# One attention unit's V products: one key tile in every key tile, in place of two in every second

## The chip, the cores and the metric

The kernel runs on one core of one Trainium2 chip. The metric is the device time of one execution in microseconds (us). The kernel before took 1166.23 us in the median of three runs (1156.73 to 1166.93).

## The reference: what is computed

The block is `x + attention(xn) + ffn(xn)` with `xn` the layer norm of `x`, which is 4 x 1024 x 128 in float32. The part that matters here is the attention:

```python
xq, xk, xv = rope(q @ Wq), rope(kv @ Wk), kv @ Wv          # q = kv = xn
xk, xv = jnp.repeat(xk, 2, axis=-1), jnp.repeat(xv, 2, axis=-1)
scores = softmax(xq @ xk * scale, axis=-1)                 # 16 heads, 1024 x 1024 each
out = (scores @ xv).transpose(0, 2, 1, 3).reshape(batch, seq_len, -1)
return out @ Wo
```

The feed-forward part (a SiLU gate with 384 hidden columns) is computed once, at the kernel's start, and is not touched.

## The kernel before, in words

**Units.** The four batches and four groups of four heads make 16 steps; a step has two halves of 512 queries. One half of one step is a unit: 32 units, numbered `u`. Units 0 to 30 run through `slot`, the last one through `last_slot`. The keys of a unit are eight key tiles `kt` of 128 keys.

**What TensorE (PE) does in a unit**, written out by hand in `slot` (L544 to L663), key tile by key tile:
- `score(kt, h)` (L554): one matmul for each head h = 0 to 3, keys in rows and queries in columns, 98 x 128 weights, 512 columns. It alternates between the two halves of `bank_s`, so it waits until ScalarE has taken the exponential of the score two before (L553).
- `maxima()` (L391): one max tile, two matmuls into `scores`, for the row maxima of the unit after this one. Sixteen of them are spread over key tiles 0 to 5. There are two places, so max tile m waits until VectorE has reduced max tile m - 2 (L388).
- `pv(u, kt, n)` (L406): the V products of one key tile. Four heads, each with weights of 128 x 32, each in its own 32 columns of the array and its own 32 partitions of `bank_o`; in the profile every head is two instructions, so one key tile has 8. They accumulate over the eight key tiles of a unit; the first waits until `bank_o` of the unit before has been read (L404).
- `denominators(u - 1)` (L416, L419) in key tile 2: eight products with ones, in the same 128 x 32 shape; `transpose_den` and `transpose_inv` (L426, L433) in key tiles 3 and 5; `project_out(u - 2)` (L442) in key tile 1; `transpose_max` (L398) in key tile 6, one 128 x 32 weight load, which waits for `o_done` (L649); and the projections of unit u + 4 (`project_chunk`, L373, and `project_v`, L381) in key tiles 6 and 7.

**Where the V products stand.** `pv_pair` runs in key tiles 0, 2, 4 and 6. In key tile 0 it issues key tiles 6 and 7 of the unit before, in 2, 4 and 6 the two key tiles just finished.

**The other engines.** ScalarE (ACT) takes 32 exponentials (L867) into `prob`, a ring of four key tiles; before it writes a ring place it waits until the V products of the key tile four before are done (L854) and until the sums that read the place are done. Between the exponentials it copies `bank_o` to `o_raw` (`read_o`, L828), `bank_m` to `y_part` (`read_y`, L845) and other things. VectorE (DVE) reduces 16 max tiles (L946), then splits the maxima (L952, L954), normalises `o_raw` (L1049, which gives `o_done`), adds two key tiles of `prob` (L1039) and rotates the projections (L937 to L941). GpSimd (POOL) splits two chunks (L1125), adds one output (L1189) and sums `prob` over key tiles in five additions (L1173, L1181). SyncE (SP) issues the DMAs; it copies a new V after `pv_done` of the unit before (L322).

Of the kernel before, what the change touches and what calls it, by code (L numbers as in the profile page):

```python
# [42 lines left out]
KT = S // 128  # L43
# [31 lines left out]
def build(nc, x, tables, w_qkv, wo_even, wo_odd, w_gu, w_down, ident_in, out):  # L75
# [10 lines left out]
    with ctx:  # L86
# [272 lines left out]
        def _(pe):  # L359
# [40 lines left out]
            def pv(u, kt, n):  # L400

                pe.wait_ge(prob_ready, NE * (KT * u + kt + 1))
                if kt == 0:
                    at_least(pe, o_read, u)  # L404
                for h in range(HG):
                    last = mm(bank_o[h * E:(h + 1) * E, :], v_sb[n][:, kt, h * E:(h + 1) * E], prob[:, kt % RING, h, :],  # L406
                              start=kt == 0, stop=kt == KT - 1)
                last.then_inc(pv_done, 1)
# [135 lines left out]
            def slot(i, j, t, last_pair):  # L544
                u, s = 4 * i + 2 * j + t, 2 * i + j
                v, w = u + 1, u + 4
                v_n, v_t = (j, 1) if t == 0 else (1 - j, 0)
                do_max = not (last_pair and j == 1 and t == 1)
                tiles = iter(range(TILES))

                def score(kt, h):

                    at_least(pe, prob_ready, NE * (KT * u + kt) + h - 1)  # L553
                    mm(bank_s[:, h % 2, :],  # L554
                       qk_pack[j][0:SCORE_K, 1, kt // QT, h, (kt % QT) * 128:(kt % QT + 1) * 128],
                       qk_pack[j][0:SCORE_K, 0, t, h, :], start=True, stop=True).then_inc(score_ready, 1)

                def pv_pair(kt):

                    if kt > 0:  # L560
                        pv(u, kt - 2, j)
                        pv(u, kt - 1, j)
                    elif not is_first(u):
                        pv(u - 1, KT - 2, j if t == 1 else 1 - j)
                        pv(u - 1, KT - 1, j if t == 1 else 1 - j)

                def maxima():
                    if do_max:
                        m = next(tiles)
                        if m < 2:  # L570

                            pe.wait_ge(rope_done, capped(2 * u + 7 + m, 2 * UNITS))
                        max_tile(v, m, v_n, v_t)

                def project_chunk(c):
                    if not last_pair:

                        pe.wait_ge(max_read, TILES * v + TILES - 1 + c // 2)
                        project(c, w, t, s + 2)


                pe.wait_ge(max_packed, 16 * u + 16)
                if isinstance(u, int) and u == 2:

                    pe.wait_ge(filled, 3)
                if do_max and t == 1:

                    pe.wait_ge(packed, 16 * PACKS * (s + 1))
                for kt in range(KT):
                    score(kt, 0)  # L590
                    if kt == 0:
                        maxima()
                        score(kt, 1)
                        maxima()
                        score(kt, 2)
                        pv_pair(kt)
                        score(kt, 3)
                        maxima()
                    elif kt == 1:
                        maxima()  # L600
                        score(kt, 1)
                        if not is_second(u):
                            project_out(u - 2, 1 - j, s - 1)
                        score(kt, 2)
                        maxima()
                        score(kt, 3)
                    elif kt == 2:
                        maxima()
                        score(kt, 1)
                        maxima()  # L610
                        pv_pair(kt)
                        if not is_first(u):
                            denominators(u - 1, 1 - t)
                        score(kt, 2)
                        maxima()
                        score(kt, 3)
                        maxima()
                    elif kt == 3:
                        if not is_first(u):
                            transpose_den(u - 1)  # L620
                        score(kt, 1)
                        maxima()
                        score(kt, 2)
                        maxima()
                        score(kt, 3)
                    elif kt == 4:
                        maxima()
                        score(kt, 1)
                        pv_pair(kt)
                        score(kt, 2)  # L630
                        maxima()
                        score(kt, 3)
                        maxima()
                    elif kt == 5:
                        if not is_first(u):
                            transpose_inv(u - 1)
                        score(kt, 1)
                        maxima()
                        score(kt, 2)
                        maxima()  # L640
                        score(kt, 3)
                    elif kt == 6:
                        pv_pair(kt)
                        score(kt, 1)
                        project_chunk(0)
                        score(kt, 2)
                        if do_max:

                            at_least(pe, o_done, u)  # L649
                            transpose_max(v)  # L650
                        project_chunk(1)
                        score(kt, 3)
                        project_chunk(2)
                    else:
                        project_chunk(3)
                        score(kt, 1)
                        if not last_pair:
                            pe.wait_ge(maxT_read, v + 1)
                            project_v(w, t, blocks=range(QT // 2))
                        score(kt, 2)  # L660
                        if not last_pair:
                            project_v(w, t, blocks=range(QT // 2, QT))
                        score(kt, 3)  # L663

            def body(i, last_pair):
# [71 lines left out]
        def _(act):  # L737
# [109 lines left out]
            def slot(i, j, t, last_pair):  # L847
                u, s = 4 * i + 2 * j + t, 2 * i + j
                first = is_first(u)
                staged = not (last_pair and (j, t) != (0, 0))  # L850
                for kt in range(KT):

                    if not (first and kt < RING):
                        act.wait_ge(pv_done, 8 * u + kt - 3)  # L854
                        if kt < 2:
                            act.wait_ge(pair_done, u)
                        elif kt == 2:
                            act.wait_ge(sum_done, 5 * u)
                        elif kt == 3:
                            act.wait_ge(den_ready, u)  # L860
                        elif kt < 6:
                            act.wait_ge(sum_done, 5 * u + 1)
                        else:
                            act.wait_ge(sum_done, 5 * u + kt - 4)
                    for h in range(HG):
                        act.wait_ge(score_ready, 32 * u + 4 * kt + h + 1)
                        A(prob[:, kt % RING, h, :], bank_s[:, h % 2, :], ACT.Exp).then_inc(prob_ready, 1)  # L867
                        if (kt, h) == (0, 2) and not first and staged:
                            stage_v(u + 3, 1 - t, s + 1 + t)
                        elif (kt, h) == (0, 3) and not first:  # L870
                            read_o(u - 1)
                        elif (kt, h) == (1, 1) and staged:
                            round_hi(0, u + 3, 1 - t, s + 1 + t)
                        elif (kt, h) == (1, 3) and not is_second(u):
                            read_y(u - 2)
                        elif (kt, h) == (2, 1):
                            if staged:
                                round_hi(1, u + 3, 1 - t, s + 1 + t)
                            if not first:
                                read_den(u - 1)  # L880
                        elif (kt, h) == (4, 1) and not first:
                            spread_inv(u - 1)
                        elif (kt, h) == (6, 2) and not (last_pair and j == 1 and t == 1):
                            read_maxT(u + 1)
# [381 lines left out]
```

## Time and profile before

| | |
|---|---|
| median of 3 runs | 1166.23 us |
| the profiled execution | 1166.15 us |
| its span | 1164.4 us |
| mean granted TensorE clock | 0.984 of full speed |
| PE busy | 1120.0 us, 96% |
| VectorE busy | 901.1 us, 77% |
| GpSimd busy | 852.9 us, 73% |
| ScalarE busy | 729.8 us, 63% |

Busy time is the union of an engine's instructions. Matmuls are pipelined and the profile models their ends, so a busy PE may still be standing between two matmuls. PEld is the loading of weights into the array, listed apart from the matmuls. In the chain of waits each piece is the time by which the end moved on; there a matmul that follows another smoothly is shorter than its own duration. "Idle before, issue" is idle time of an engine in which it waited for no semaphore that the profile shows.

### The profile page before, as it was taken

The numbers are of one execution on the slowest core, as the hardware profiler recorded it, in microseconds if no ns is written. First come the engines' busy times: TensorE is split into PE (matmuls) and PEld (weight loads), VectorE is DVE, ScalarE is ACT, GpSimd is POOL, SyncE is SP. The second block draws the span as 40 slices with busy tenths as digits, with TensorE's granted clock in tenths as the row PEclk, the third lists the DMA queues.
The fourth block names the chain that finished last, engine by engine and source line by source line (L and its number), as shares of the span: only waits on it lengthen the run. The fifth ranks groups of instructions, "written<-read, shape, count | busy, mean of one in ns | idle before, by whom it ended". The sixth has DMA issues, their size and how long they took to land.

```text
span 1164.4 us, 17086 instructions
## 1 busy us (share of the span) xinstructions
PE 1120.0 (96%) x6288; PEld 663.2 (57%) x6288; DVE 901.1 (77%) x1023; ACT 729.8 (63%) x1327; POOL 852.9 (73%) x268
## 2 busy tenths in 40 slices
PE   5899899999999999999999999999999999999997
PEld 4787455655565555556565555555555555554443
DVE  7686877787887877788787877778787877776655
ACT  3234666666676666666676666666676666665564
POOL 3222868788788778888788778887778878887660
PEclk9899999999999999999999999999999999998889
DMA  6662908062340718062341718072341618050000
GB/s 230 159 258 77 256 2 224 1 205 58 85 141 19 207 37 224 2 205 57 96 129 26 201 37 224 1 210 53 96 130 30 196 37 224 1 130 1 5 1 19
DMA packets 56338, 124.98 MB, mean 107 GB/s; under 512 B 8000, under 2 KB 19520, under 8 KB 54080
## 3 DMA queue, kind: packets, MB, share of 16 engines
q1 hardware_dynamic: 56256, 123.90, 36.8%
q8 instruction: 51, 0.84, 0.3%
q14 instruction: 31, 0.25, 0.1%
HBM read 53.08 MB, written 10.49 MB: 55 GB/s over the span
## 4 chain that ended last, share of the span: by engine, by line
PE 79%; DVE 14%; SPq 2%; ACT 2%; issue 1%; DMA 1%; POOL 0%; DVEq 0%; ACTq 0%; POOLq 0%
PE bank_o L406 20%; PE bank_s L554 18%; PE scores L391 17%; DVE row_max L946 12%; PE scores L373 7%; PE bank_m L381 3%; PE bank_m L442 2%; PE bank_m L416 2%; PE bank_m L419 2%; SPq L239 2%; PE scores L492 2%; PE bank_s L509 1%; ACT prob L867 1%; PE bank_o L509 1%; DVE stats L961 1%
## 5 line engine op out<-in xcount | busy, mean ns | idle before, releaser
L946 DVE TENSOR_REDUCE row_max<-scores 128x1 f32<-128x1024 f32 x512 | 597.1, 1214 | 206.8 <-PE scores L391 206.5
L867 ACT ACTIVATE prob<-bank_s 128x512 f32<-128x512 f32 x992 | 576.7, 600 | 252.9 <-PE bank_s L554 229.5
L1181 POOL TENSOR_TENSOR prob_sum<-prob_sum,prob 128x2048 f32<-128x2048 f32 x93 | 425.7, 4577 | 13.5 <-ACT prob L867 0.5
L554 PE MATMUL bank_s<-qk_pack 98*128 98x512 f32 x992 | 415.8, 434 | 7.1 <-ACT prob L867 3.1
L391 PE MATMUL scores<-qk_pack 96*128 96x512 f32 x1024 | 337.5, 411 | 8.9 <-DVE row_max L946 0.3
L554 PEld LDWEIGHTS bank_s<-qk_pack 98*128 98x128 f32 x992 | 186.9, 189 | 184.9 <-issue 84.7
L406 PE MATMUL bank_o<-prob,v 128*32 128x512 f32 x2048 | 253.0, 612 | 0.0
L391 PEld LDWEIGHTS scores<-qk_pack 96*128 96x128 f32 x1024 | 179.5, 190 | 74.5 <-DVE row_max L946 53.0
L1181 POOL TENSOR_TENSOR prob_sum<-prob_sum,prob_pair 128x2048 f32<-128x2048 f32 x31 | 142.7, 4602 | 101.7 <-DVE prob_pair L1039 101.7
L1125 POOL TENSOR_TENSOR qk_stage<-rope,qk_stage 128x512 fp32r<-128x512 f32 x64 | 81.8, 1279 | 92.3 <-ACT qk_stage L753 92.3
L1173 POOL TENSOR_TENSOR prob_sum<-prob 128x2048 f32<-128x2048 f32 x31 | 142.2, 4586 | 0.0
L406 PEld LDWEIGHTS bank_o<-prob,v 128*32 128x32 f32 x2048 | 54.0, 110 | 123.1 <-issue 69.1
L373 PE MATMUL scores<-x_stage,w_stage 128*128 128x512 f32 x336 | 98.6, 401 | 0.0
L834 ACT COPY den<-bank_m 128x512 f32<-128x512 f32 x31 | 18.2, 586 | 86.6 <-PE bank_m L419 86.6
L1039 DVE TENSOR_TENSOR prob_pair<-prob 128x2048 f32<-128x2048 f32 x31 | 70.8, 2285 | 0.0
L373 PEld LDWEIGHTS scores<-x_stage,w_stage 128*128 128x128 f32 x336 | 61.4, 189 | 14.5
L1189 POOL TENSOR_TENSOR y_acc<-y_part,y_acc 128x512 f32<-128x512 f32 x31 | 39.5, 1274 | 26.5 <-ACT y_part L845 26.5
L381 PEld LDWEIGHTS bank_m<-w_stage,x_stage 128*128 128x128 f32 x336 | 46.3, 191 | 3.6
L937 DVE TENSOR_TENSOR scores<-scores,table 128x512 f32<-128x512 f32 x64 | 44.2, 691 | 2.5 <-PE scores L373 2.5
L941 DVE TENSOR_TENSOR rope<-scores,rope 128x512 f32<-128x512 f32 x64 | 44.3, 692 | 2.2
L939 DVE TENSOR_TENSOR rope<-scores,table 128x512 f32<-128x512 f32 x64 | 43.6, 681 | 0.6 <-PE scores L373 0.5
L381 PE MATMUL bank_m<-w_stage,x_stage 128*128 128x128 f32 x336 | 43.8, 266 | 0.0
(105 smaller groups left out, 742.4 us busy)
## 6 DMA issues: line engine op xcount, KB each, us to landing
qk_pack<-qk_stage SPq DMA_DIRECT2D x384, 128.0 KB, 5.0
table<-tables SPq DMA_DIRECT2D x16, 2048.0 KB, 9.6
w_stage<-w_scratch SPq DMA_DIRECT2D x14, 640.0 KB, 4.5
v<-v_stage SPq DMA_DIRECT2D x32, 256.0 KB, 8.1
xT_scratch<-xT_hl SPq DMA_DIRECT2D x4, 1024.0 KB, 9.5
x_stage<-xT_scratch SPq DMA_DIRECT2D x4, 1024.0 KB, 7.0
w_scratch<-w_split SPq DMA_DIRECT2D x1, 2560.0 KB, 15.1
x_all<-x SPq DMA_DIRECT2D x4, 512.0 KB, 11.7
```

Of the source, the lines that this page charges most:

```text
L373: last = mm(scores[:, c, :], w_from[:, a, c, :], x_from[:, r, cols], start=n == 0, stop=n == 2)
L381: last = mm(bank_m[:, j * 128:(j + 1) * 128], x_from[:, r, at:at + 128], w_from[:, a, 4, :], start=n == 0, stop=n == 2)
L391: last = mm(scores[:, 2 * (m % places) + c, :], qk_pack[n][0:SPLIT_K, 0, t, h, (m % QT) * 128:(m % QT + 1) * 128], qk_pack[n][0:SPLIT_K, 1 ...
L406: last = mm(bank_o[h * E:(h + 1) * E, :], v_sb[n][:, kt, h * E:(h + 1) * E], prob[:, kt % RING, h, :], start=kt == 0, stop=kt == KT - 1)
L554: mm(bank_s[:, h % 2, :], qk_pack[j][0:SCORE_K, 1, kt // QT, h, (kt % QT) * 128:(kt % QT + 1) * 128], qk_pack[j][0:SCORE_K, 0, t, h, :], s ...
L867: A(prob[:, kt % RING, h, :], bank_s[:, h % 2, :], ACT.Exp).then_inc(prob_ready, 1)
L941: V.tensor_tensor(rope[:, 2 * k, :], scores[:, 2 * k, :], rope[:, 2 * k + 1, :], ALU.add).then_inc(rope_done, 1)
L946: V.tensor_reduce(row_max[:, m:m + 1], scores[:, at:at + 2, :].rearrange("p c k -> p (c k)"), axis=AX.X, op=ALU.max).then_inc(max_read, 1)
L1039: V.tensor_tensor(prob_pair[:], prob[:, 4 % RING], prob[:, 5 % RING], ALU.add).then_inc(pair_done, 1)
L1125: TT(qk_stage[:, 2 * k + 1, t, :], rope[:, 2 * k, :], qk_stage[:, 2 * k, t, :].bitcast(F32), ALU.subtract).then_inc(lo_done, 1)
L1173: TT(prob_sum[:, t], prob[:, 0], prob[:, 1], ALU.add).then_inc(sum_done, 1)
L1181: TT(prob_sum[:, t], prob_sum[:, t], part, ALU.add).then_inc(sum_done, 1)
```

## The change

`pv_pair` becomes `pv_next`, and it stands in every key tile. In key tiles 2 to 7 it issues the V products of the key tile two before; in key tiles 0 and 1 those of key tiles 6 and 7 of the unit before. `read_o` moves from after the exponential of (key tile 0, head 3) to after (key tile 1, head 3), behind `read_y`. The last unit (`last_slot`) stays as it is.

```diff
@@ -555,14 +555,12 @@
                        qk_pack[j][0:SCORE_K, 1, kt // QT, h, (kt % QT) * 128:(kt % QT + 1) * 128],
                        qk_pack[j][0:SCORE_K, 0, t, h, :], start=True, stop=True).then_inc(score_ready, 1)
 
-                def pv_pair(kt):
-
-                    if kt > 0:
+                def pv_next(kt):
+
+                    if kt > 1:
                         pv(u, kt - 2, j)
-                        pv(u, kt - 1, j)
                     elif not is_first(u):
-                        pv(u - 1, KT - 2, j if t == 1 else 1 - j)
-                        pv(u - 1, KT - 1, j if t == 1 else 1 - j)
+                        pv(u - 1, KT - 2 + kt, j if t == 1 else 1 - j)
 
                 def maxima():
                     if do_max:
@@ -593,7 +591,7 @@
                         score(kt, 1)
                         maxima()
                         score(kt, 2)
-                        pv_pair(kt)
+                        pv_next(kt)
                         score(kt, 3)
                         maxima()
                     elif kt == 1:
@@ -602,13 +600,14 @@
                         if not is_second(u):
                             project_out(u - 2, 1 - j, s - 1)
                         score(kt, 2)
+                        pv_next(kt)
                         maxima()
                         score(kt, 3)
                     elif kt == 2:
                         maxima()
                         score(kt, 1)
                         maxima()
-                        pv_pair(kt)
+                        pv_next(kt)
                         if not is_first(u):
                             denominators(u - 1, 1 - t)
                         score(kt, 2)
@@ -621,12 +620,13 @@
                         score(kt, 1)
                         maxima()
                         score(kt, 2)
+                        pv_next(kt)
                         maxima()
                         score(kt, 3)
                     elif kt == 4:
                         maxima()
                         score(kt, 1)
-                        pv_pair(kt)
+                        pv_next(kt)
                         score(kt, 2)
                         maxima()
                         score(kt, 3)
@@ -637,10 +637,11 @@
                         score(kt, 1)
                         maxima()
                         score(kt, 2)
+                        pv_next(kt)
                         maxima()
                         score(kt, 3)
                     elif kt == 6:
-                        pv_pair(kt)
+                        pv_next(kt)
                         score(kt, 1)
                         project_chunk(0)
                         score(kt, 2)
@@ -660,6 +661,7 @@
                         score(kt, 2)
                         if not last_pair:
                             project_v(w, t, blocks=range(QT // 2, QT))
+                        pv_next(kt)
                         score(kt, 3)
 
             def body(i, last_pair):
@@ -867,12 +869,12 @@
                         A(prob[:, kt % RING, h, :], bank_s[:, h % 2, :], ACT.Exp).then_inc(prob_ready, 1)
                         if (kt, h) == (0, 2) and not first and staged:
                             stage_v(u + 3, 1 - t, s + 1 + t)
-                        elif (kt, h) == (0, 3) and not first:
-                            read_o(u - 1)
                         elif (kt, h) == (1, 1) and staged:
                             round_hi(0, u + 3, 1 - t, s + 1 + t)
-                        elif (kt, h) == (1, 3) and not is_second(u):
-                            read_y(u - 2)
+                        elif (kt, h) == (1, 3) and not first:
+                            if not is_second(u):
+                                read_y(u - 2)
+                            read_o(u - 1)
                         elif (kt, h) == (2, 1):
                             if staged:
                                 round_hi(1, u + 3, 1 - t, s + 1 + t)
```

## Rows read from the trace of the kernel before

**Rows 1.** The page: busy time; chain of waits by engine; two groups (mean ns | idle)

```profile
PE 1120.0 (96%) x6288; PEld 663.2 (57%) x6288; DVE 901.1 (77%) x1023; ACT 729.8 (63%) x1327; POOL 852.9 (73%) x268
...
PE 79%; DVE 14%; SPq 2%; ACT 2%; issue 1%; DMA 1%; POOL 0%; DVEq 0%; ACTq 0%; POOLq 0%
...
L946 DVE TENSOR_REDUCE row_max<-scores 128x1 f32<-128x1024 f32 x512 | 597.1, 1214 | 206.8 <-PE scores L391 206.5
L867 ACT ACTIVATE prob<-bank_s 128x512 f32<-128x512 f32 x992 | 576.7, 600 | 252.9 <-PE bank_s L554 229.5
```

**Rows 2.** Windows, one unit: us, busy us (x instructions) by engine, clock, DMA share, GB/s

```profile
535.30:568.00 32.70, 32.41 (x189) 18.92 (x188) 26.41 (x28) 21.93 (x41) 26.75 (x9) 1.00 0.00 1
```

**Rows 3.** The chain in order of time, one unit: start us, us, what

```profile
563.21 0.70 PE scores L373 x3
...
569.64 0.38 PE bank_s L554
...
570.51 0.23 PE bank_s L554
570.74 1.85 PE bank_o L406 x16
572.60 0.43 PE bank_s L554
573.02 0.47 PE scores L391 x2
...
576.03 0.71 PE bank_s L554 x2
...
577.46 0.62 PE scores L391 x2
...
579.93 0.86 PE bank_m L416 x8
...
582.59 2.37 DVE row_max L946 x2
...
585.00 0.74 PE scores L391 x2
...
586.21 0.65 PE scores L391 x2
...
592.36 0.73 PE scores L391 x2
...
601.20 0.63 PE bank_s L554 x2
```

**Rows 4.** Timeline, a pair, a score before a late max tile: start us, us, instruction [idle]

```profile
570.67 0.16 PEld L406 LDWEIGHTS bank_o<-prob,v 128*32 128x32 f32 x8 [0.35 <-ACT prob L867]
...
572.53 0.19 PEld L554 LDWEIGHTS bank_s<-qk_pack 98*128 98x128 f32 x1 [0.84 <-issue]
...
584.46 0.40 PE L554 MATMUL bank_s<-qk_pack 98*128 98x512 f32 x1
```

**Rows 5.** Waits on weight loads and matmuls: us in total, times, longest

```profile
PEld bank_s L554 <- issue: 84.7, 120, 1.7
```

**Rows 6.** Timeline of PE in the last unit: one key tile of V products, then sums

```profile
1151.47 1.06 PE L406 MATMUL bank_o<-prob,v 128*32 128x512 f32 x8
1152.35 1.04 PE L717 MATMUL bank_m<-prob,ones 128*32 128x512 f32 x8
```

**Rows 7.** Timeline from the last max tile to the transpose of the maxima

```profile
559.74 0.73 PE L391 MATMUL scores<-qk_pack 96*128 96x512 f32 x2
...
561.98 0.88 DVE L952 CAST max_hl<-row_max 128x16 fp32r<-128x16 f32 x1
...
563.00 0.69 DVE L1049 TENSOR_TENSOR o_norm<-o_raw,bank_m 128x512 f32<-128x512 f32 x1
...
563.98 0.27 PE L398 MATMUL bank_m<-ident,max_hl 128*32 128x128 f32 x1
563.98 0.53 PEld L373 LDWEIGHTS scores<-x_stage,w_stage 128*128 128x128 f32 x3
```

**Rows 8.** Timeline of ScalarE and GpSimd in key tiles 1 to 4

```profile
576.80 0.58 ACT L845 COPY y_part<-bank_m 128x512 f32<-128x512 f32 x1
...
581.41 4.59 POOL L1173 TENSOR_TENSOR prob_sum<-prob 128x2048 f32<-128x2048 f32 x1
```

## The prediction

> **What bounds the kernel now.** I read the page first, for which engine is full. TensorE (PE) is busy 96% of the span and makes 79% of the chain of waits; the 14% under DVE are pieces of the max-tile reduction L946 [rows 1]. VectorE, by contrast, stands 206.5 us waiting for max tiles [rows 1]. So PE sets the time, and VectorE only here and there. The windows say the same of one unit: 32.70 us, of which PE is busy 32.41, VectorE 26.41, GpSimd 26.75 and ScalarE 21.93, at full granted clock [rows 2]. Thirty-one such units are 1014 us of the span, and they are what the change touches.
>
> Then I read the chain in order of time, because a busy PE hides two kinds of loss there. In it a smooth score is 0.23 us and a smooth max tile 0.47, a pair of V products is 1.85, and eight more products in the same shape behind it add 0.86 [rows 3].
>
> *Loss one, the switch of shape.* Two key tiles of V products at the rate of those 0.86 would be 1.72, and the pair shows 1.85: 0.13 at its entry. The score behind it takes 0.43 in place of 0.23: 0.20 at its exit [rows 3]. The timeline shows why. The 128x32 weights of the pair are loaded at 570.67, when the score in front is all but over (570.74), and the score's 128-column weights behind it at 572.53, after 0.84 us in which the loader waited for nothing the profile names [rows 4]; the pair ends at 572.60 [rows 3]. Between two full-array matmuls that load is hidden. It happens behind every such block: 120 times, 84.7 us in all [rows 5], about four in each unit. One block of V products costs PE 0.33 us beside its own work.
>
> *Loss two, the waits.* After the pairs VectorE has nothing to reduce, then gets max tiles faster than it can take them. A max tile then waits for a place and costs 0.74 or 0.73 in place of 0.47, with 0.14 of standing before it (a score's end at 584.86 [rows 4] to 585.00); others show 0.62 and 0.65, and scores that follow each other too closely 0.71 and 0.63 for two and 0.38 for one [rows 3]. Above the smooth prices these are 0.41 + 0.40 + 0.15 + 0.18 + 0.25 + 0.16 + 0.15 = 1.7 us, with 0.1 of small ones 1.8 us a unit. This is all that a better order can give back.
>
> **The change, part by part.**
>
> *1. Four blocks become eight.* The V products are the same 8 instructions for each key tile, 0.86 us. But a unit now enters and leaves the shape eight times, not four (the denominators still stand right behind the block of key tile 2). That is 4 x 0.33 = 1.32 us a unit; unit 0 has no V products of a unit before it, so it gets three more, and the sum is 30 x 4 + 3 = 123 blocks x 0.33 = +41 us. Nothing hides it, since it is PE's own time. No row of a main unit shows a single block. The nearest is in the last unit, where one key tile takes 1.06 us as modelled and the next block starts 0.88 after it [rows 6]: no cheaper body than half a pair. A lower bound is the transpose of the maxima, also 128x32 but with 128 columns: the weights of the matmul behind it load from its very start, 563.98 [rows 7], so a switch there costs nothing seen. An upper bound is 0.5, if the loads of a lone block are exposed for each of its two halves (0.13 more). I take 0.33, from rows of the very same instructions.
>
> The Trainium skill, "TensorEngine Tiling (Array Packing)", Key Properties, says that changing the tiling mode, not merely the tile, drains the array: it speaks against this change. The row at 572.53 agrees and the row at 563.98 does not show it. "TensorE: Matmul & The Clock Gate", Part 2, puts a pipe drain at about 128 cycles; as an estimate from that page two drains at full clock are 0.11 us a block, so 13 us in place of 41 and, with the other terms below, no difference; the rival of the cheap switch stands at that place with a price from rows.
>
> *2. Waits given back.* I walked one unit through the new order with the smooth prices above, 0.60 for an exponential [rows 1], 1.17 for a reduction in a row of them (half of 2.37 [rows 3]), 0.04 from a release to the start behind it (582.59 + 2.37 to 585.00 [rows 3]), and 0.27 more for a matmul that PE had to stand for (0.74 less 0.47). From key tile 3 on, with 0.99 of V products in every key tile, a max tile comes 2.9 us or more behind the one but one before it, save two places with 2.1, and two reductions are 2.34: VectorE keeps up, and the stops of 0.4 shrink to 0.1 in all. Before the first score of key tile 2 there now stands a V product and a max tile: the close pair of 0.71 loses its 0.25. What stays is the start of the unit (0.16), the second score of key tile 0 (0.15), and the same place in key tiles 2 and 4: it needs the exponential of the score two before, so it ends 0.04 + 0.60 + 0.04 + 0.50 = 1.18 after that score, while PE's own work there is score, max tile, score, 0.93, which is a stop of 0.25 each. Together 0.9 in place of 1.8: -0.9 us a unit, -28 us.
>
> *3. A new stop at the transpose of the maxima.* It waits for the normalisation, which ends 1.71 after the split begins (561.98 to 563.69 [rows 7]). Before, the end of the last max tile (559.74 + 0.73 = 560.47) and that release lay 3.2 us apart, and PE had 0.23 + 0.23 + 1.85 + 0.43 + 0.70 + 0.23 = 3.7 us of work between, so it did not stop. In the new order the last max tile stands behind the V products, its reduction starts at once, and the release is 1.17 + 1.71 and some 0.1 between, 3.0 us, after it. PE's work between has one key tile less of V products: 3.7 - 0.86 = 2.8. It stops for some 0.15, and with the restart of 0.27 this is 0.4 us a unit: +12 us. If the reduction before the last is late, it is 0.7; if the split is earlier than I think, nothing.
>
> *4. read_o one key tile later, behind read_y.* The first V product of a unit (key tile 2) waits for it. Two copies of 0.58 [rows 8] behind the exponential (1, 3) end some 1.0 us after it; PE meanwhile has a score, a max tile and their waits. In the walk the copy ends about 0.05 us before it would stop PE. I put it at nothing; its cover is the max tile in front of the block. Late by 0.5 it would be 15 us. Behind it on ScalarE stand the exponentials (2, 0) and (2, 1), 0.5 to 0.8 later; the scores that wait for them stand behind the V products and denominators, over 2.5 us of PE's work. The second rounding and so GpSimd's chain start 0.8 later: its first addition, 581.41 to 586.00 [rows 8], frees the ring place for key tile 4. In the walk the exponential (4, 0) waits 0.15 for it, and no score waits for that. At nothing.
>
> *5. Ring, V buffers, DMA.* The V products of a key tile are still done one key tile or more before the ring place is written. SyncE's copy of V waits for the last product of the unit before, now some 4 us later in the unit, where its queue is busy with other issues. At nothing.
>
> **The sum.** +41 - 28 + 12 = +25 us, 0.8 us a unit. The profiled execution took 1166.15 us, within 0.1 of the median, so the forecast of the median is 1166 + 25 = **1191 us**.
>
> **The rivals.**
> - *The forecast*, the switches paid in full and about half of the waits given back; with 0.3 us a unit either way, 1182 to 1200. Chance 0.57.
> - *The even feed pays for the switches* (faster). The place is the stops of key tiles 3 and 5 and the close scores, 1.8 us a unit. For it speaks that VectorE waits 206.5 us for PE [rows 1], most of it behind bunched V products. If all stops go and none comes at the transpose, a unit is 1.32 - 1.8 = -0.5, which gives 1151 us. It decides once more than 1.3 us a unit come back. Against it: the distance of one exponential remains in three key tiles. Chance 0.12.
> - *A lone block switches cheaply*, 0.11 a block, between the row at 563.98 and that at 572.53: 123 x 0.11 = 14, and 14 - 28 + 12 = -2, 1164 us, no difference. Against it is the row at 572.53. Chance 0.12.
> - *No wait is given back*, because the copy of the sums or the ring stops PE as often as the max tiles did: +41 without the transpose's stop, 1207 us, and with it 1219. For it: the 0.05 us of margin in point 4. Chance 0.13.
> - Something between, slower by under 1%: 0.06.
>
> About 1% is what a measurement of this kernel can tell from no change. Slower by more than that are the forecast and the case of no wait given back, 0.70; within it the cheap switch and the small loss, 0.18; faster 0.12. The range reaches down to the cheap switch, 1162, and up to the lower end of the worst case, 1208, and leaves out the rest of these two and the faster case; the likeliest case alone is 1182 to 1200.
>
> **What would show it.** In the chain of the changed kernel a single block of V products should be 0.99 and the matmul behind it 0.20 above its smooth price; the weight loads behind it should show an unnamed idle time about 240 times, not 120. The pieces of 2.37 under DVE should be gone or rarer. The transpose L398 should wait for the normalisation in most units, not now and then. A window of a unit should be 33.3 to 33.7 us. I am wrong if a lone block is under 0.9 with a smooth successor, if units are 32.7 or less, or if the first V product of a unit waits for the copy of the sums.

## The result and the profile after

The changed kernel took 1209.46 us in the median of four runs (1206.5 to 1211.45), against 1165.34 for the kernel before with a fourth run of its own: a ratio of 1.039, 95% interval 1.034 to 1.044, about +45 us (40 to 51). The forecast was slower, 1191 us, range 1162 to 1208. The sign is right; the loss is nearly twice the 25 us forecast and lies just past the range.

The page of the changed kernel (span 1206.5 us; the profiled execution took 1208.29), first line as in [rows 1], then the same two groups. Lines past L590 have moved by two: L946 is now L948, L952 is L954, L1049 is L1051.

```profile
PE 1141.8 (95%) x6288; PEld 655.3 (54%) x6288; DVE 932.7 (77%) x1023; ACT 741.2 (61%) x1327; POOL 853.7 (71%) x268
...
L948 DVE TENSOR_REDUCE row_max<-scores 128x1 f32<-128x1024 f32 x512 | 601.1, 1219 | 219.9 <-PE scores L391 219.8
L869 ACT ACTIVATE prob<-bank_s 128x512 f32<-128x512 f32 x992 | 580.5, 599 | 302.0 <-PE bank_s L554 282.0
```

PE is busy for 22 us more, but the span grew by 42: the other half is time in which PE stands. The transposes L398 come one a unit, so the distance from one to the next is the length of a unit. Its median is 34.43 us against 32.64 before: 1.79 us a unit, where 0.8 were forecast. The 26 units between the third transpose and the 29th take 46.5 us more than before; the start and the end of the program give 4 us back. A window of 34.00 us (columns as in [rows 2]), a little less than a unit, holds 32.88 us of PE:

```profile
535.00:569.00 34.00, 32.88 (x185) 18.27 (x183) 26.98 (x28) 21.84 (x40) 26.23 (x9) 1.00 0.33 91
```

The chain in order of time, one unit, answers to [rows 3].

```profile
570.03 1.00 PE bank_o L406 x8
571.03 0.66 PE scores L391 x2
...
572.16 0.47 PE scores L391 x2
572.63 0.48 PE bank_s L554
573.12 0.99 PE bank_o L406 x8
574.11 0.43 PE bank_s L554
...
578.31 0.68 PE scores L391 x2
578.99 0.02 issue
579.01 1.24 DVE row_max L948
580.25 0.02 issue
580.27 1.76 DVE max_hl L954
582.03 0.02 issue
582.05 0.06 DVE max_hl L956
582.12 0.04 issue
582.16 0.70 DVE o_norm L1051
582.86 0.04 issue
582.90 0.28 PE bank_m L398
...
589.66 0.50 PE bank_s L554
...
597.39 0.49 PE bank_s L554
597.89 0.63 PE scores L391 x2
```

A lone block of V products is 0.99 to 1.00, and what follows it is 0.43 for a score and 0.66 for a max tile, 0.20 above smooth: the 0.33 of the prediction. The pieces of 2.37 under DVE are gone. The second score of key tile 4 (572.63) stops for 0.25, as walked. Those of key tiles 0 and 2 (589.66, 597.39) stop for 0.27 and 0.26, and one max tile (597.89) for 0.16. What was not foreseen is the end of the unit's max tiles: from the last of them (ends 578.99) to the transpose the chain runs over VectorE for 3.9 us, where I had 3.0, and 1.76 of it is one copy of 16 columns.

The waits of the changed kernel (us in total, times, longest) name it too: all 29 are in different units. The kernel before had 1.4 us there, in two units (three idle times, since the loader's and PE's own are counted apart).

```profile
PEld bank_m L398 <- DVE o_norm L1051: 44.1, 29, 2.2
PE bank_m L398 <- DVE o_norm L1051: 31.6, 29, 1.8
```

Next to GpSimd the copy explains itself. Timeline of the changed kernel:

```profile
572.66 9.32 POOL L1183 TENSOR_TENSOR prob_sum<-prob_sum,prob 128x2048 f32<-128x2048 f32 x2
...
580.27 1.75 DVE L954 CAST max_hl<-row_max 128x16 fp32r<-128x16 f32 x1
```

GpSimd's additions of key tiles 2 and 3 end at 572.66 + 9.32 = 581.98, the copy at 582.02. One unit elsewhere (297.16 + 9.33 = 306.49, copy 304.77 + 1.76 = 306.53) shows the same 0.04. And so did the kernel before: its addition ended at 558.24 + 4.58 = 562.82, and the copy [rows 7] at 561.98 + 0.88 = 562.86.

```profile
558.24 4.58 POOL L1181 TENSOR_TENSOR prob_sum<-prob_sum,prob 128x2048 f32<-128x2048 f32 x1
```

The copy has no length of its own there; it ends when GpSimd does. This holds for every copy of over 0.25 us: 28 of the 32 before and 27 in the changed kernel, and each of them ends 0.03 to 0.04 us behind one of GpSimd's additions. The median of all 32 went from 0.878 to 1.756 us, the shortest is 0.174 in both.

### The profile page after: what moved, and what is told of

Same layout as the page of the kernel before. It is cut to its first block, busy times and chain, and to the rows that moved or that the text cites. A ratio compares the mean times of both kernels' runs of the same rounds, so it can differ in the third digit from the quotient of the medians.

```text
span 1206.5 us, 17086 instructions
## 1 busy us (share of the span) xinstructions
PE 1141.8 (95%) x6288; PEld 655.3 (54%) x6288; DVE 932.7 (77%) x1023; ACT 741.2 (61%) x1327; POOL 853.7 (71%) x268
## 4 chain that ended last, share of the span: by engine, by line
PE 86%; DVE 11%; ACT 1%; issue 1%; POOL 1%; DMA 1%; ACTq 0%; DVEq 0%; POOLq 0%
PE scores L391 22%; PE bank_s L554 21%; PE bank_o L406 19%; PE scores L373 6%; DVE max_hl L954 4%; PE bank_m L381 3%; DVE row_max L948 3%; PE bank_m L419 2%; PE bank_m L416 2%; PE bank_m L442 2%; PE scores L492 2%; DVE o_norm L1051 2%; PE bank_s L509 1%; PE bank_m L426 1%; PE bank_m L433 1%
## 5 line engine op out<-in xcount | busy, mean ns | idle before, releaser
L948 DVE TENSOR_REDUCE row_max<-scores 128x1 f32<-128x1024 f32 x512 | 601.1, 1219 | 219.9 <-PE scores L391 219.8
L554 PE MATMUL bank_s<-qk_pack 98*128 98x512 f32 x992 | 410.6, 435 | 2.9 <-ACT prob L869 1.7
L406 PE MATMUL bank_o<-prob,v 128*32 128x512 f32 x2048 | 273.6, 608 | 0.0
L391 PEld LDWEIGHTS scores<-qk_pack 96*128 96x128 f32 x1024 | 182.5, 191 | 109.8 <-DVE row_max L948 83.8
L406 PEld LDWEIGHTS bank_o<-prob,v 128*32 128x32 f32 x2048 | 40.9, 108 | 78.6 <-issue 39.8
L954 DVE CAST max_hl<-row_max 128x16 fp32r<-128x16 f32 x32 | 48.2, 1506 | 1.1
```

The costliest lines, as they stand in the source:

```text
L391: last = mm(scores[:, 2 * (m % places) + c, :], qk_pack[n][0:SPLIT_K, 0, t, h, (m % QT) * 128:(m % QT + 1) * 128], qk_pack[n][0:SPLIT_K, 1 ...
L554: mm(bank_s[:, h % 2, :], qk_pack[j][0:SCORE_K, 1, kt // QT, h, (kt % QT) * 128:(kt % QT + 1) * 128], qk_pack[j][0:SCORE_K, 0, t, h, :], s ...
L948: V.tensor_reduce(row_max[:, m:m + 1], scores[:, at:at + 2, :].rearrange("p c k -> p (c k)"), axis=AX.X, op=ALU.max).then_inc(max_read, 1)
L954: V.tensor_copy(max_hl[:, 0, :].bitcast(F32R), row_max[:]).then_inc(max_hi, 1)
```

## The experiments

Two theories. **Lock** (L in the expectations): VectorE's copy is held until GpSimd's third addition ends, and the change made GpSimd's chain late, since its second split waits for a rounding that now stands behind read_y and read_o. **Switches** (S): the eight blocks are all of it, and PE would stop for something else anyway. Each set ran beside the kernel before on its own chip (medians 1159 to 1162 there), so ratios are compared.

**a_round: GpSimd's chain early again.**

```diff
 elif (kt, h) == (1, 1) and staged:
     round_hi(0, u + 3, 1 - t, s + 1 + t)
+    round_hi(1, u + 3, 1 - t, s + 1 + t)
 ...
 elif (kt, h) == (2, 1):
-    if staged:
-        round_hi(1, u + 3, 1 - t, s + 1 + t)
```

> The changed kernel with ScalarE's second rounding of a unit moved from after exponential (2, 1) to (1, 1), right behind the first. Theory L (lock): VectorE's copy of the row maxima is held until GpSimd's third addition has ended, and GpSimd is late since its second split waits for a rounding that now stands behind read_y and read_o. Then GpSimd's additions start about 3 us earlier in the unit, the copy takes 0.2 us in place of 1.76, the transpose of the maxima stops PE no more (29 stops of 1.1 plus a restart of 0.2 each, 38 us), and the kernel takes about 1171 us. Theory S (the switches alone cost more than 0.33 each, and PE would stop for the next thing anyway): the copy may shorten, but the time stays within 10 us of the changed kernel's 1209.

Measured: 1170.81 us against 1160.31, ratio 1.009 (1.007 to 1.012). The eight blocks and the late read_o are all still there, and 3.0% of the 3.9% is gone. A unit is 33.10 us in the median, 1.33 less than in the changed kernel, and when the matmuls of the two kernels are laid side by side from one transpose to the next, all of the 1.33 lies at the transpose and at the matmul right behind it. Timeline of this kernel: the addition before ends at 564.13, the copy takes 0.17 (0.174 to 0.176 in all units), and the transpose does not wait.

```profile
559.54 4.59 POOL L1182 TENSOR_TENSOR prob_sum<-prob_sum,prob 128x2048 f32<-128x2048 f32 x1
565.65 0.17 DVE L953 CAST max_hl<-row_max 128x16 fp32r<-128x16 f32 x1
566.77 0.10 PEld L398 LDWEIGHTS bank_m<-ident,max_hl 128*32 128x32 f32 x1
```

**a_swap: the normalisation ahead of the split.**

```diff
+                    if not is_first(u):
+                        normalise(u - 1)
                     split_max(u + 1)
                 else:
                     invert(u - 1)
-                if not is_first(u):
                     normalise(u - 1)
```

> The changed kernel with VectorE's normalisation in front of the split of the maxima, not behind it. Theory L: the normalisation (0.69) runs while GpSimd's addition still holds the copy up, so the transpose is released about 0.66 us earlier; with 29 stops this is -19 us, 1190 us, and the copy still ends where GpSimd's third addition ends. If the copy is long by itself and not for GpSimd, it stays 1.76 long wherever it starts and the time stays near 1209.

Measured: 1193.08, ratio 1.029 (1.027 to 1.031), a gain of 1.0% or 12 us where 19 were expected. The copy starts later and is shorter, yet ends in the same place, 0.03 behind GpSimd (567.40 + 9.32 = 576.72):

```profile
567.40 9.32 POOL L1184 TENSOR_TENSOR prob_sum<-prob_sum,prob 128x2048 f32<-128x2048 f32 x2
...
574.86 0.68 DVE L1051 TENSOR_TENSOR o_norm<-o_raw,bank_m 128x512 f32<-128x512 f32 x1
...
575.45 1.30 DVE L954 CAST max_hl<-row_max 128x16 fp32r<-128x16 f32 x1
```

The normalisation, with one operand in PSUM, ran its usual 0.68 beside the addition. The transpose's wait shrank from 1.54 to 1.01 and the unit from 34.43 to 33.92, so by 0.5 and not by 0.66. The chain gives the same: from the end of the copy to the transpose it has 0.87 in the changed kernel (582.03 to 582.90) and 0.35 here. In the changed kernel the subtraction adds only 0.06 there, since the normalisation starts before it is over; here it stands last and counts in full.

```profile
576.78 0.18 DVE max_hl L956
576.97 0.14 issue
577.11 0.27 PE bank_m L398
```

The copy started later by the normalisation and still ended with GpSimd, so its length is GpSimd's doing.

**b_late_o: read_o alone.** The kernel before, with its pairs.

```diff
-elif (kt, h) == (0, 3) and not first:
-    read_o(u - 1)
 ...
-elif (kt, h) == (1, 3) and not is_second(u):
-    read_y(u - 2)
+elif (kt, h) == (1, 3) and not first:
+    if not is_second(u):
+        read_y(u - 2)
+    read_o(u - 1)
```

> The kernel before, pairs and all, with read_o alone moved to behind read_y at (1, 3). No switch is added. Theory L: GpSimd's first addition starts 0.5 to 1.0 us later in the unit, the copy of the maxima ends as much later, and the transpose, which had some 0.1 to 0.4 us to spare, stops PE for 0.4 to 0.7 us: +12 to +20 us, 1178 to 1186. Theory S: nothing, 1166.

Measured: 1176.57, ratio 1.014 (1.012 to 1.016), +16 us without one added switch. The copy's median is 1.378, and the transpose waits in 27 units, where it waited in two:

```profile
567.53 1.39 DVE L952 CAST max_hl<-row_max 128x16 fp32r<-128x16 f32 x1
569.80 0.10 PEld L398 LDWEIGHTS bank_m<-ident,max_hl 128*32 128x32 f32 x1 [0.55 <-DVE o_norm L1049]
```

A unit is 33.14 us in the median, 0.50 more than before. Not all of it stands at the transpose: 0.26 lies in front of it, 0.07 right behind it, and 0.16 at the second max tile of the unit that follows (0.65 in the chain, where the kernel before has 0.49), whose weights wait 0.23 us for a rotation on VectorE (L941).

**b_split: the switches alone.** Each pair of the kernel before is parted by one score or max tile in its own key tile; here key tile 0.

```diff
                         score(kt, 2)
-                        pv_pair(kt)
+                        pv_one(kt, 0)
                         score(kt, 3)
+                        pv_one(kt, 1)
                         maxima()
```

> The kernel before with each pair of V products split in its own key tile by one score or max tile between them; read_o stays where it was. This is the switch by itself: 123 more blocks at 0.33 are +41 us, 1207 us, less what a slightly more even feed of VectorE gives back (up to 10 us), plus no stop at the transpose. If a lone block switches cheaply (0.11), it is +14, 1180. If the loads of a lone block cost more than I took (0.5), it is +62, 1228.

Measured: 1193.61, ratio 1.030 (1.027 to 1.034), +35 us: 41 less some 6 from the feed, within what was said. Its unit is 33.81 us, 1.17 more than before, where four switches alone are 1.32. No unit waits at the transpose, the copy's median is 0.388, and both stops of 2.37 are still in the chain. In it the blocks cost what they cost in the changed kernel:

```profile
572.93 1.00 PE bank_o L406 x8
573.93 0.43 PE bank_s L554
574.36 0.99 PE bank_o L406 x8
575.35 0.89 PE scores L373 x3
```

The projection behind the second is 0.89 against 0.70 [rows 3]: again 0.2.

**a_reduce_hi: the copy in another form.**

```diff
-V.tensor_copy(max_hl[:, 0, :].bitcast(F32R), row_max[:]).then_inc(max_hi, 1)
+V.tensor_reduce(max_hl[:, 0, :].bitcast(F32R), row_max[:].unsqueeze(2), axis=AX.X, op=ALU.max).then_inc(max_hi, 1)
```

> The changed kernel with the first instruction of the split of the maxima, a copy from SBUF to SBUF, written as a reduction over an axis of one element: same input and output, one input, another form. It asks what holds the copy up. If only the copy's form is held while GpSimd's addition runs, the reduction takes some 0.2 us, the subtraction behind it 0.18, and the transpose is released 1.5 us earlier: about 1171 us, as a_round. If the subtraction with its two inputs from SBUF is held too, it takes over the wait (some 1.5 us long, ending with GpSimd's third addition) and the time stays at 1209 or a little under.

Measured: 1201.70, ratio 1.036 (1.032 to 1.039), the second of the two outcomes. The reduction is never held (0.169 to 0.172 in all units); the subtraction behind it takes the wait over, with a median of 1.552, and ends 0.03 after GpSimd (570.52 + 9.31 = 579.83):

```profile
570.52 9.31 POOL L1183 TENSOR_TENSOR prob_sum<-prob_sum,prob 128x2048 f32<-128x2048 f32 x2
578.13 0.17 DVE L954 TENSOR_REDUCE max_hl<-row_max 128x16 fp32r<-128x16 f32 x1
578.33 1.53 DVE L956 TENSOR_TENSOR max_hl<-row_max,max_hl 128x16 f32<-128x16 f32 x1
```

**b_round_swap: would the kernel before gain?** Both moves of a_round and a_swap on the kernel before.

> The kernel before, pairs and read_o in place, with ScalarE's second rounding moved up to (1, 1) and VectorE's normalisation in front of the split. In the kernel before the transpose hardly waited (3 stops, 1.4 us), so both theories give little: 1166 less 0 to 3 us. The copy should be 0.2 us in every unit. If it is faster by more than 5 us, another wait hung on GpSimd's chain that the trace of before did not show.

Measured: 1170.34, ratio 1.008 (1.005 to 1.010): slower, a miss for both theories, though the copy is short in every unit (0.164 to 0.174), as said. The chain shows what the early rounding ran into. Two roundings now follow each other on ScalarE, and the exponential that PE waits for stands behind them; two units:

```profile
576.69 1.14 ACT qk_stage L753 x2
577.83 0.51 ACT prob L867
578.34 0.04 issue
578.38 0.50 PE bank_s L554
...
609.60 1.16 ACT qk_stage L753 x2
```

In front of the first of them the chain names a DMA that frees the roundings' buffer (it landed at 576.69), but that is not the cause. ScalarE never stands idle there: in every middle unit the rounding starts right behind the exponential (1, 1). In every second unit, as at 609.60, the last such DMA landed over 11 us earlier, and PE loses the same. Laid beside the kernel before, PE comes 0.46 us later to this score in each of 26 units, and 0.17 of it comes back within the unit, which is 32.94 us against 32.64. No time is lost or won at the transpose, where the swap acts; so the rounding's place explains the loss, though the swap was not run alone. In a_round the roundings stand at the same place and cost nothing against the changed kernel, which has a block of V products in key tile 1 and read_o further on.

**three and three_swap: fewer, longer blocks.** Key tiles 0 to 2 in key tile 3, 3 to 5 in key tile 6, 6 and 7 with the denominators in key tile 1. read_y, read_o, the second rounding and one max tile move as well, so these runs do not show the blocks alone.

```diff
                             transpose_den(u - 1)
                         score(kt, 1)
                         maxima()
+                        pv_block(0)
 ...
-                        pv_pair(kt)
+                        pv_block(3)
```

> The opposite of the change: three blocks of V products a unit in place of four. Key tiles 0, 1, 2 stand in key tile 3, key tiles 3, 4, 5 in key tile 6, key tiles 6 and 7 of the unit before at the end of key tile 1 with the denominators behind them; read_y moves to (1, 2), read_o to (1, 3), the second rounding to (1, 1). By the price of a switch, 30 x 0.33 = -10 us. By the bunching (VectorE idle behind longer blocks, max tiles then too fast for it) the stops of 1.8 us a unit could grow; but there are two long blocks among the max tiles in place of three, so VectorE's idle time falls from 6.2 to about 3.5 us a unit and I expect the stops to shrink by 0.3 to 1.0: 1130 to 1150 us against 1166. If an even feed is what matters, it is slower than before.

> The kernel of three blocks with the normalisation in front of the split as well. With three key tiles of V products in front of the transpose it is not late, so the same time as three within 3 us.

Measured: 1192.64 and 1192.15, ratios 1.028 (1.023 to 1.032) and 1.026 (1.022 to 1.030). A clear miss, by some 40 us. The switches are saved, since three key tiles in one block take 2.71, that is 3 x 0.86 and 0.13 once. More was lost to stops, of a kind that I had not counted: behind three key tiles of V products ScalarE has no score in stock, and PE waits for two exponentials in a row, from 568.81 to 570.04.

```profile
564.94 2.71 PE bank_o L406 x24
...
568.81 0.02 issue
568.83 0.51 ACT prob L865
569.34 0.04 issue
569.39 0.61 ACT prob L865
```

ScalarE's waits for scores went from 229.5 to 357.7 us. The swap changed nothing, as said.

**hybrid6, hybrid5, shift4: between the two.** The pair of key tile 0 stays, and so does read_o. Which of the unit's own key tiles (in brackets) stand in which key tile:

```text
before    2: (0, 1), 4: (2, 3), 6: (4, 5)
hybrid6   2: (0,), 3: (1,), 4: (2,), 5: (3,), 6: (4, 5)
hybrid5   2: (0,), 3: (1,), 4: (2,), 6: (3, 4, 5)
shift4    2: (0,), 4: (1, 2), 6: (3, 4, 5)
```

> Six blocks of V products a unit: the pair of key tile 0 and the pair of key tile 6 stay as they were before, and only the two pairs between become single key tiles in key tiles 2 (with the denominators), 3, 4 and 5. read_o stays at (0, 3), so GpSimd's chain and the transpose of the maxima are as before. Two more switches are +0.66 us a unit. The two stops of 0.4 for max tiles and the smaller ones of key tile 4 go (1.0 us), the second score of key tile 4 keeps its stop. Net -0.3 us a unit, 1150 us where before is 1159: slightly faster. If stops and switches balance, no difference; if the stops are not given back, +20 us.

> Five blocks: as hybrid6, but key tile 3's products join the block of key tile 6, which then has three. One more switch than before (+0.33 us a unit) and none of V products in key tile 5, so VectorE is behind there and one stop of 0.4 stays: no difference from before, within 6 us.

> Four blocks as before, other sizes: the pair of key tile 0, one key tile in key tile 2 with the denominators, two in key tile 4, three in key tile 6. No switch is added or removed. The longest gap of VectorE is 0.86 shorter, but 0.86 us of PE's work has also left the stretch of the max tiles, so VectorE has less time to catch up: I expect no difference from before (within 8 us), faster if the bunch at key tile 2 alone makes the stops.

Measured: ratios 1.000 (0.998 to 1.003), 1.000 (0.998 to 1.002) and 1.001 (0.998 to 1.003), from eleven to twelve runs each. For hybrid5 and shift4 that was expected. hybrid6 was expected 0.8% faster and is not: its unit is 32.63 us, as before. Its chain has two blocks more and no piece of DVE in the unit, so the late max tiles cost nothing any more. But two other stops grew. The second max tile of a unit takes 0.64 where it took 0.49, and the second score of key tile 4 takes 0.49 where it took 0.30:

```profile
570.90 0.64 PE scores L393 x2
...
587.60 0.49 PE bank_s L556
```

The stops that went are the 1.0 us that were counted; the two that grew take 0.34 back, and 0.66 for two switches takes the rest.

shift4 shows the other side of the lock. Its copy is held as long as in the changed kernel, 1.742 us in the median, and it costs nothing: the transpose waits in three units only. Here three key tiles of V products stand between the last max tile and the transpose; in the changed kernel it is one.

## Why the prediction was wrong

- **Point 1, the switches: right.** 0.33 a block, 123 blocks, 41 us; the price shows in every chain, and b_split measured +35 with the feed included.
- **Point 2, waits given back: right in sum, by places that partly differ.** Points 1 and 2 together gave +13 us, 0.42 a unit. a_round, which has both and hardly a stop at the transpose, is 0.94% (0.72 to 1.16) slower, 0.46 a unit. The stops left in the chain of the changed kernel are 0.27 + 0.26 + 0.25 + 0.16 = 0.94, where 0.9 were walked; the start of the unit has none of them, and the second score of key tile 0 has 0.27 in place of 0.15.
- **Point 3, the new stop at the transpose: right in place, wrong in size. This is the step that failed.** It was put at 0.4 us a unit, 12 us, 0.7 at most. The trace shows 1.1 of standing and 0.2 of slow restart in 29 units, 38 us, and a_round takes 3.0% or 35 us away with it. The working took 1.71 from the split's start to the normalisation's end as VectorE's own time. But 0.88 of it was the copy, and that copy was already waiting for GpSimd: its end is GpSimd's end plus 0.04. The clue stood in the trace, a copy of 16 columns at 0.88 beside a subtraction of the same 16 columns at 0.18. So the release hangs on GpSimd's third addition, not on VectorE's last reduction.
- **Point 4, "at nothing": wrong, and it made the larger part of that stop.** The first V product indeed did not wait for the copy of the sums. But I followed GpSimd's chain only to the ring place of key tile 4, and not on to its third addition. Before, that addition ended 2.35 us behind the last max tile (560.47 to 562.82) and the release, the end of the normalisation, 3.2; in the changed kernel it is 2.99 (578.99 to 581.98) and 3.9. Forecast was 3.0. PE's work in between is 3.7 before and 2.8 after, as forecast. Of the 1.1 us of standing, 0.65 is the addition that comes later; the other 0.4 is the key tile of V products that PE no longer has there, 0.86, less the 0.45 by which it was late enough before. b_late_o, which moves read_o and nothing else, costs 16 us.
- **The sign of 240 unnamed idle times of the weight loads: the count was misread.** Of the 120 in [rows 5] only 92 are the 0.84 in front of a load behind a block; 27 are of 0.16 and stand elsewhere, and 31 loads behind blocks are not among the 120, since their 0.84 stands beside the name of an exponential. That 120 comes near the number of blocks is chance. In the changed kernel the scores show 60, because 95 loads of scores have their 0.84 beside an exponential's name and 92 blocks are followed by a max tile, with [0.84 <-DVE row_max L948]. Counted by size, under every name, such loads went from 123 to 246: the twice as many that the sign meant.
- In numbers: 41 - 28 + 35 = +48, measured +45 (40 to 51).

What the lock is, the Trainium skill says in "SBUF — State Buffer", "Who interferes with whom": a VectorE copy or cast in a 2-port mode, and a VectorE instruction with two SBUF inputs against a GpSimd instruction that reads SBUF, contend for a port pair, and whoever comes second is blocked until the first is done; a reduction never contends. The runs agree for each form: copy held, subtraction with two SBUF inputs held, reduction at 0.17 and the normalisation from PSUM at 0.68 not held. No row of the profile shows the mode in which the copy ran, nor the ports; the runs show the forms and the times.

Still open: why the transpose of the maxima, with weights as narrow as those of the V products, shows no price of a switch.

## What to carry to other kernels

When an instruction in a trace is several times longer than one of its size beside it, its duration may be a wait, and an edit that moves either engine changes it; look for what ends just before it does, here 0.03 to 0.04 us. Such a wait costs nothing as long as the engine behind it has other work (shift4), so its length has to be held against that work. Alternating TensorE between 128x32 products and full-width ones costs at each block, here 0.33 us, so spreading such products pays only if each block removes a stop of that size. Moving a copy on one engine has to be followed to the last instruction of every chain behind it, not to the first deadline; and the exponentials queued behind it are part of that (b_round_swap).

## What the hardware showed that was not expected

A VectorE copy of 128 x 16 from SBUF to SBUF, 0.17 us when free, was held up to 1.78 us in the changed kernel, until a GpSimd addition of 4.6 us had ended; a subtraction of the same size with both inputs in SBUF was held up to 1.57 us, a one-input reduction never. The profile shows the whole of it as the instruction's duration and none as idle time before it. The 128x32 transpose of 128 columns (L398) shows neither of the two costs of the V products, 0.11 in the chain when it does not wait, though its weights have the same width; why was not tried.
